# First edge layer: the 392-column one-hots of the degree counts made by ScalarE in two passes

## What is computed

```python
h = relu(layernorm(x))
x = x + relu(segment_sum((h[dst] @ weight[type]), src, 50000) + bias)   # first layer
h = relu(layernorm(x))
h_sparse = top32_per_row(h @ W_neigh)
deg = segment_sum(ones, dst, 50000)
x = x + h @ W_self + segment_sum(h_sparse[src], dst, 50000) / max(deg, 1)  # second layer
```

## Time and profile before

| | |
|---|---|
| median of 3 runs | 4215.76 us (4210.98 to 4216.35) |
| profiled execution, its own time | 4204.39 us |
| its span, first to last instruction | 4202.7 us |
| DVE busy over the span | 3252.2 us, 77% |
| PE busy | 2852.9 us, 68% |
| POOL busy | 2229.0 us, 53% |
| ACT busy | 1941.7 us, 46% |
| first edge layer | about 363 to 1800 us |

### The profile page before, as it was taken

How to read it: one execution, slowest core, us unless ns; L and a number is a source line. 1 busy time by engine, 2 the same in 40 slices (tenths; PEclk the granted TensorE clock), 3 DMA queues, 4 the chain that set the end, 5 groups by cost and what they waited for, 6 DMA issues and landing times.

```text
span 4202.7 us, 74312 instructions
## 1 busy us (share of the span) xinstructions
PE 2852.9 (68%) x10746; PEld 1759.7 (42%) x10747; DVE 3252.2 (77%) x14070; ACT 1941.7 (46%) x5805; POOL 2229.0 (53%) x1609
## 2 busy tenths in 40 slices
PE   2555766677888888867777777777764666556655
PEld 1224655555666666633333333333333344333332
DVE  8998788888888888759999999999994333333333
ACT  0001333333333333347777777777764555555553
POOL 0004876667777777745555555555543334333332
PEclk7997888889999999988888888888886767778777
DMA  9402567665555555534444444444434555555553
GB/s 353 176 0 49 90 134 150 148 145 102 102 101 101 101 102 99 101 94 158 160 160 160 155 159 153 156 157 160 160 128 148 151 151 156 156 150 151 150 150 115
DMA packets 307274, 576.87 MB, mean 137 GB/s; under 512 B 32005, under 2 KB 187944, under 8 KB 307214
## 3 DMA queue, kind: packets, MB, share of 16 engines
q1 hardware_dynamic: 211598, 419.86, 29.9%
q0 software_dynamic: 95616, 156.31, 19.5%
HBM read 317.16 MB, written 258.88 MB: 137 GB/s over the span
## 4 chain that ended last, share of the span: by engine, by line
DVE 44%; issue 22%; PE 14%; DVEq 10%; DMA 6%; POOL 4%; ACT 1%; POOLq 0%; SPq 0%; ACTq 0%
DVE zone_c L1127 11%; PE banks L1479 7%; DVE best L1122 6%; DVEq L1144 5%; DMA agg<-msg,sidx 4%; DVE zone_c L1152 4%; PE banks L1386 3%; DVE zone_c L1134 3%; DVE zone_c L835 2%; DVEq L1152 2%; DVE zone_c L1020 2%; DVE zone_c L1024 2%; DVE zone_c L831 2%; DVE zone_c L1022 2%; DVE zone_c L833 2%
## 5 line engine op out<-in xcount | busy, mean ns | idle before, releaser
L1462 PE MATMUL banks<-w,hT 128*128 128x512 f32 x1568 | 835.4, 694 | 191.2 <-ACT hT L1250 191.2
L1479 PE MATMUL banks<-zone_c 128*128 x1568 | 616.9, 555 | 428.9 <-DVE zone_c L1152 362.8
L1152 DVE SCALAR_TENSOR_TENSOR zone_c<-banks,rdeg,zone_c 128x256 f32 x784 | 379.1, 484 | 651.9 <-issue 246.8
L653 POOL DMA_INDIRECT agg<-msg,sidx x400 | 658.0, 1645 | 224.3 <-issue 111.2
L641 POOL DMA_INDIRECT rows_in<-in_x,gidx x400 | 435.6, 1089 | 480.5 <-DVE gidx L882 350.1
L1479 PEld LDWEIGHTS banks<-zone_c 128*128 128x128 f32 x1568 | 384.7, 274 | 661.5 <-issue 612.3
L713 POOL DMA_INDIRECT zone_c<-hs,gidx x392 | 373.0, 952 | 495.3 <-PE banks L1479 442.2
L1127 DVE MATCH_REPLACE8 zone_c<-best,zone_c 128x256 f32<-128x256 f32 x1568 | 624.3, 410 | 0.0
L1462 PEld LDWEIGHTS banks<-w,hT 128*128 128x128 f32 x1568 | 339.2, 222 | 631.8 <-issue 521.0
L1122 DVE MAX8 best<-zone_c 128x8 f32<-128x256 f32 x1568 | 548.4, 413 | 4.3
L1267 ACT ACTIVATE zone_c<-zone_c,ones 128x128 f32<-128x128 f32 x784 | 312.0, 398 | 467.7 <-PE banks L1479 459.3
(11 more groups left out here) (220 smaller groups left out, 4840.0 us busy)
## 6 DMA issues: line engine op xcount, KB each, us to landing
out_rows<-zone_c SPq DMA_DIRECT2D x196, 512.0 KB, 2.7
agg<-bias SPq DMA_DIRECT2D x2, 25344.0 KB, 102.9
zone_c<-agg SPq DMA_DIRECT2D x98, 512.0 KB, 4.6
hs<-zone_c SPq DMA_DIRECT2D x98, 512.0 KB, 3.0
zone_c<-out_rows SPq DMA_DIRECT2D x98, 512.0 KB, 4.0
rows_in<-in_x SPq DMA_DIRECT2D x97, 512.0 KB, 3.7
keyrow<-key_rows SPq DMA_DIRECT2D x100, 320.0 KB, 3.8
zone_c<-bucket_rows SPq DMA_DIRECT2D x25, 512.0 KB
```

The lines of the kernel that those rows point to most:

```text
L653: pool.indirect_dma_start(out=agg[:, :], out_offset=bass.IndirectOffsetOnAxis(ap=sidx[p][:, j:j + 1], axis=0), in_=msg[p][:, j * D:(j + 1) ...
L1152: v.scalar_tensor_tensor(to, bank[k][:, 0:D], rdeg8[:, bass.ds(word // 1024, 1)], to, ALU.mult, ALU.add).then_inc(summed, 1)
L1462: last = mm(bank[4 + j][:, :], hT[p][:, c, j * P:(j + 1) * P], w1[:, c, :], start=(c == 0), stop=(c == KC - 1))
L1479: mm(bank[k][:, 0:D], hot1[:, k, :], ring[:, bass.ds(word % RING, 1), :].rearrange("p o d -> p (o d)"), start=True, stop=True).then_inc(st ...
```

## The change

ScalarE makes `one_high` in two passes through a new scratch tile `near_high` (f16, laid over `act_junk`). `highcol` holds the negated column number. DVE no longer makes `one_high`. The new function `edge0_buckets` runs at the end of ACT's step b for group b + 2, and twice ahead of the loop. PE waits for `bucket_hot` as well ahead of the first degree matmul of a group, and DVE waits for it before it overwrites `highcol`.

```diff
@@ act_junk = sb("act_junk", [P, B, D])
+        near_high = act_junk[:, :, :].rearrange("p j d -> p (j d)").bitcast(F16).rearrange(
+            "p (j d) -> p j d", j=B)[:, :, 0:TILES]
@@ DVE, edge0_front(b, r, p)
                 wait_from(dve, sidx0, b - 1, b, 2)
+                wait_from(dve, bucket_hot, b - 1, b, 2)
                 v.tensor_copy(lowcol[p][:, :], low7[:, bass.ds(b * B, B)])
-                v.tensor_copy(highcol[p][:, :], bucket[:, bass.ds(b * B, B)])
+                v.tensor_scalar(highcol[p][:, :], bucket[:, bass.ds(b * B, B)], -1.0, None, ALU.mult)
...
                 wait_from(dve, degrees0, b - 1, b, 2)
                 for j in range(B):
-                    v.tensor_scalar(one_low[p][:, j, :], iota_h[:, 0:P], lowcol[p][:, j:j + 1], None, ALU.is_equal)
-                    last = v.tensor_scalar(one_high[p][:, j, :], iota_h[:, 0:TILES], highcol[p][:, j:j + 1],
-                                           None, ALU.is_equal)
+                    last = v.tensor_scalar(one_low[p][:, j, :], iota_h[:, 0:P], lowcol[p][:, j:j + 1], None,
+                                           ALU.is_equal)
                 last.then_inc(node_hot, 1)
@@ ACT
+            def edge0_buckets(b, p):
+
+                act.wait_ge(col0, b + 1)
+                wait_from(act, degrees0, b - 1, b, 2)
+                wait_from(act, bucket_hot, b, b, 1)
+                for j in range(B):
+                    last = nc.scalar.activation(near_high[:, j, :], iota_h[:, 0:TILES], ACT.Abs,
+                                                bias=highcol[p][:, j:j + 1])
+                last.then_inc(bucket_near, 1)
+                act.wait_ge(bucket_near, b + 1)
+                for j in range(B):
+                    last = nc.scalar.activation(one_high[p][:, j, :], near_high[:, j, :], ACT.Relu,
+                                                bias=ones[:, 0:1], scale=-1.0)
+                last.then_inc(bucket_hot, 1)
+
             def edge0_step(b, r, p):
...
                 edge0_evict(b, p, 3)
+                if front:
+                    edge0_buckets(b + 2, p)

             edge0_front(0, 0)
+            edge0_buckets(0, 0)
+            edge0_buckets(1, 1)
             edge0_turned(0, 0, 0)
@@ PE, edge0_degree(b, p, j)
                 if j == 0:
                     pe.wait_ge(node_hot, b + 1)
+                    pe.wait_ge(bucket_hot, b + 1)
```

More of the change, by code:

```diff
@@ L375, in graph_layers @@
         node_hot = sem("node_hot")
+        bucket_near = sem("bucket_near")
+        bucket_hot = sem("bucket_hot")
         degrees0 = sem("degrees0")
```

## The result

The changed kernel takes **4222.15 us** (median of 11 runs, 4217.35 to 4229.57) where the kernel before takes 4216.07 us (median of 11, 4209.0 to 4220.62). The ratio is 1.002, with a 95% interval of 1.0011 to 1.0029. Close to 90 us of work left the busiest engine, and the kernel is 6 us slower.

A forecast was written before the change was run, and what follows sets the result against it. A ring of DVE and PE waiting for each other, through ACT's square root, was taken as the bound, not busy DVE. 9.5 - 7 + 0 + 1.4 + 2 = +6 us on the 4215.8 median gave 4222 us, range 4203 to 4262.

The forecast's parts named there:

- the likeliest case: Passes covered, a small cost on the ring; chance 0.58, own range 4205 to 4236 us.
- the ring: Sort phase: square root, DVE's work through sort_hots, PE's sort_place to tile 2, ACT's evict, next square root; 13.15 us.
- half-clock groups: Sort-phase groups where PE runs at 1.2 GHz after a stand: 21, 1.46 us each; 5 fewer, 7 us back.
- What bounds the kernel: Sort phase: DVE and PE wait for each other around the ring; one_high lies beside it, its branch level, gaining nothing.
- The passes: ACT: eight passes of 392 columns a group, 607 ns each, both rounds 4.31 us, bounds 3.3 and 5.2.
- 0.17 us a group on the ring: Sort phase: degree matmul no longer inside PE's wait; 13.15 becomes 13.32 us, 9.5 us over 56 groups.
- Rank phase: Its ring runs over a DMA; later evict covered by 0.9 us, 0 in the sum, about 14 us without cover.
- Hist and rest: 8 hist groups cost 1.4 us; last three steps, without a PE side job, 2 us, bounds 0 and 4.
- ACT late: Slower rival: passes over 4.4 us, excess one to one onto the ring; 4252 to 4286 us; chance 0.28.
- DVE as the bound: Faster rival: DVE's relief counts in the sort phase down to POOL's floor, 24 us, 4192 us; chance 0.08.
- POOL's 13.17 us: Sort phase: time of POOL's four gathers and adds a group, taken as the floor for shorter groups.
- The half-clock groups did not vanish: Faster rival: PE keeps its clock with its stand moved; 31 us less 13 us of cost, 4198 us; chance 0.06.

The follow-up runs named there:

- e1: Kernel before with one_high filled with ones once and never made again by DVE or ACT; 4215.42 us, ratio 0.9997.
- e9: Changed kernel with sort_hot signalled by tile, in four steps a group, PE waiting for its tile's step; 4222.88 us, ratio 1.0015.
- e3: Changed kernel with the Abs round moved ahead of the evict of tile 2, Relu round left in place; 4213.29 us, ratio 0.9994.
- e13: Changed kernel with one more ACT pass per group, of 24 columns; 4230.30 us, ratio 1.0033.
- e7: Changed kernel with a ninth full ACT pass per group; 4314.96 us, ratio 1.0239.
- e12: Changed kernel with Abs round ahead of the first turned copy, square root ahead of the evict of tile 2, sort_hot by tile; 4171.91 us, ratio 0.9895.
- e11: Changed kernel with the Abs round ahead of the evict of tile 2 and sort_hot signalled by tile; 4173.89 us, ratio 0.9906.
- e5: Kernel before with ACT's square root moved ahead of the evict of tile 2; 4198.22 us, ratio 0.9957.
- e10: Kernel before with sort_hot signalled by tile, four times a group; 4185.42 us, ratio 0.9930.
- e4: Changed kernel with ACT's square root moved ahead of the evict of tile 2; 4222.87 us, ratio 1.0015.
- e2: Kernel before plus ACT's eight passes into a scratch tile; DVE still makes one_high, PE doesn't wait for the passes; 4211.52 us, ratio 0.9988.

## Why the prediction was right

The predicted 4222 us is the measured 4222.15, and the likeliest case is the one that came: a small cost on the ring, part of it paid back by fewer half-clock groups. That the number agrees to 0.2 us is luck, as the account at the end of this section shows. Step by step:

**What bounds the kernel: right.** Two level branches around a ring, with `one_high` beside it. e1 shows it: 0.92 us a group is taken from DVE, the plain group gets 0.09 us shorter, and DVE waits longer instead. Of the forecast for the changed profile, DVE's wait in plain groups (1.2 to 1.4 us) was measured at 1.36, its busy time (90 us or so down) at 86.6 down.

**The passes: right.** 607 ns was the estimate; the medians are 613 ns (Abs) and 606 ns (Relu):

```profile
L1197 ACT ACTIVATE act_junk<-iota_h,highcol x400: 604/613/627, 369.1 to 1791.9; 128x392 f16<-128x392 f16 x134
L1202 ACT ACTIVATE zone_c<-act_junk,ones x400: 604/606/622, 371.3 to 1794.1; 128x392 f16<-128x392 f16 x134
```

Both rounds took 4.35 us, where the sum had 4.31. The second round starts 0.03 us after the first ends (1206.41 against 1204.22 + 2.16). Passes without a wait between them overlap by 0.09 us, so ACT's wait on itself costs 0.12 us. The sum had 0.09 of that in it, since it set the rounds end to end. There is still the one table load of 1283 ns at the start, as the earlier trace rows had it.

**0.17 us a group on the ring: 0.22 measured.** The place was right. The degree matmul, no longer inside the wait, takes 0.16 us of the ring (the legs under e9), and e3 takes the loss away. The passes' end is as level with `sort_hots` as the prediction put it (7.80 against 7.79 us). What it left out is the way from the passes' end to PE's start: 0.14 us, where the earlier trace rows show 0.06 from DVE to PE.

**Half-clock groups: right sign, but the size was a guess between wide bounds, and its reason didn't hold.** The sum gave 7 us back for 5 fewer of 21. By the granted clock the phase had 20 before and has 13 now. Of the 52 groups 7 fewer are slow, at 1.4 us each 10 us, against 52 x 0.22 = 11 us on the ring. The sort phase came out 1.2 us longer, not 2.5. The prediction took fewer on the condition that these groups keep their spacing in time. They don't: they came two to four groups apart before, and come five apart now, 68 us. What is kept is the mean group (below), and it was luck that the guess lay near.

**Rank phase, nothing: held within what can be told.** From the first to the last matmul of that side job the kernel before took 375.9 us and the changed one 379.1. e1, which has no passes, took 379.2, and e3 and e9, which have them, 376.0 and 375.8. The 3.2 us is no more than the scatter of this phase.

**Hist and rest: mis-sized, the term of the sum that failed.** I put 1.4 us for hist and 2 us, at most 4, for the last steps; the tail is 9.5 us longer. The groups with no side job have no one-hots to wait for, so nothing covers the 4.35 us there. In the tail the distances between square roots were 11.56, 11.95 and 11.50 us before and are 12.48, 13.98 and 13.88 now, and the rest of the 9.5 us lies behind the last one. ACT and PE, in the changed kernel:

```profile
1778.63 2.16 ACT L1202 ACTIVATE zone_c<-act_junk,ones 128x392 f16<-128x392 f16 x4
1780.93 0.48 PE L1361 MATMUL banks<-zone_c 128*128 128x392 f16 x1 [2.70 <-DVE zone_c L905]
1782.06 1.91 PE L1410 MATMUL banks<-w,hT 128*128 x4
```

The wait is booked on DVE's `one_low`, which had long been done; ACT's last pass ends at 1780.79 (1778.63 + 2.16). PE stands 2.7 us here and then runs at the lower clock level, so this group loses twice. So does the one ahead of it. The first one, with the same stand, keeps its clock and loses 0.92 us. PE stood and fell to the lower level in the tail before too, ahead of its folds; the granted clock of the tail goes from 0.93 to 0.88. Late hist groups take about 13.9 instead of 12.8 us, which looks like the same loss. There it was made up for by one early group, 13.15 us where it was 17.72. Its cause is open: e3, which has no loss in late hist, has the 17.72 us again, and its rank phase still starts only 0.7 us earlier than the changed kernel's.

So the sum was +9.5 - 7 + 0 + 1.4 + 2 = +6, and the layer's account is +1 in the sort phase, +9.5 in the tail and +1 ahead: 12 us in the profiled pair, where the medians show 6. The profiled execution of the kernel before was 12 us below its median, and that of the changed kernel 2 us. Which stages make up for the missing 6 us in the medians is open, since each kernel has one trace. The forecast of 4222 us came out although a term of 2 us was in truth 9.5.

**The rivals.** ACT late was near: between 0.23 and 0.51 us more on the ring was enough (e13, e7). e7 shows that I had it far too cheap, at 36 to 70 us, where the ninth pass alone brought 93. The point from which it decides was wrong too: not 0.1 us over my 4.31, but where the plain group passes an edge between 13.60 and 13.88 us. DVE as the bound is refuted by e1's plain groups. POOL's 13.17 us, the floor of that rival, was no fixed cost: the mean group of e12 is 12.90 us. The Trainium skill, "Perfetto Trace Analysis", Optimizing Scalar/DVE Operations, says offloading may make sense when DVE is saturated. At 88% busy it brought nothing here until both rings were open (e11), and 12 us then. The half-clock groups did not vanish with the passes' new place. e5 and e10 reach what that rival was priced for in another way, with PE off the ring.

## What to carry to other kernels

Before work is moved from a busy engine, follow the ring: which wait ends each group, and is the work on it? Here an engine that was 88% busy and stopped once a group was not the bound, and its relief was worth nothing until the wait was gone. Work put "two groups ahead" in a program's terms is as early as the instruction it stands behind; ask when the consumer comes, above all in the stages where nothing else covers it. Judge a change by the undisturbed iteration as well as by the total, which can hide half a microsecond an iteration. Where PE stands and then runs at the lower clock on the ring, try to take PE off the ring (a finer signal, an earlier small instruction) before shortening anything.

## What the runs showed of the hardware

**The mean group time held at 13.64 to 13.66 us** in eight kernels whose plain groups took from 12.65 to 13.60 us. The share of groups with a half-clock stretch moved to fill the difference: 33, 18, 17, 17, 11, 10, 9 and 3 of 52 (e4, before, e1, e3, changed, e9, e2, e13). These groups come in a regular pattern: two of every three in e4, every fifth in the changed kernel, and 23 apart in e13. In each pattern the mean comes to 13.65 us, as (4 x 13.37 + 14.76) / 5 in the changed kernel and (22 x 13.60 + 14.85) / 23 in e13. Saving and loss of half a microsecond a group were both invisible in the length of the phase. In all eight kernels PE stands 1.8 to 2.6 us a group in the mean and is on the path that sets the next group. In e5, e10 and e11 the clock falls in 18, 21 and 14 of the 52 groups, about as often as before, but PE is not on that path, and the mean follows the plain groups (12.93 to 13.32 us). In e12 it doesn't fall.

**Past that mean the loss is a jump.** At 13.88 us (e7) the clock falls in nearly each group, and the mean is 15.13 us. The Trainium skill, "TensorE: Matmul & The Clock Gate", HAM oscillation, describes a loop in which PE's wait makes the clock fall anew in every round. The traces agree that it falls after a stand, and in e7 in 44 of 52 rounds. In the eight kernels above PE stands in every round as well, and the clock falls in 3 to 33 of 52. What decides in which group it falls is not settled by these runs; they varied the length of the group and PE's place on the path.
